# Large transfers moved to ACT's DMA queue, casting loads cut into pieces, in a transformer block on 8 cores

## The chip, the cores and the metric

One Trainium2 chip, 8 cores, the same program on each. Each core has its own 2 of the 16 sequences and its own copy of the weights; there is no exchange between cores. The metric is device microseconds of the slowest core. TensorE (PE), its weight load (PEld), VectorE (DVE), ScalarE (ACT), GpSimd (POOL) and SyncE (SP) each run their own instructions in order; SP only issues transfers. Sixteen DMA engines per core move the data.

## What is computed

One layer on x of [16, 2048, 1024] in float32:

```python
qkv = einsum('btc,fc->btf', x, w_qkv)                  # 16 heads of 64
p = softplus(einsum('bhqd,bhkd->bhqk', q, k) / 8)
p = p * p * causal
attn = p / (sum(p, -1) + 1e-9)
x = layernorm(x + einsum('btc,oc->bto', attn @ v, w_proj) + b_proj)
h = gelu(lora(x, quant(W_fc), b_fc, A_fc, B_fc))       # 1024 -> 4096
x = layernorm(x + lora(h, quant(W_proj), b_proj, A_proj, B_proj))
```

`quant` rounds a weight to 8 bits by its largest absolute value, and `lora` adds 2 * (x A^T) B^T. The kernel merges the LoRA product into the rounded weight.

## The kernel before

**Two halves.** The first half is attention for both sequences of a core, output projection and first layernorm (LN). The second is the FFN, matmul behind matmul on PE. In the first half the work goes by units: a unit is one block of keys against 512 queries for a pair of heads. Scores go to PSUM (L740), ACT applies softplus (L751), POOL masks the diagonal blocks (L758), DVE squares (L766), and the AV matmuls (L790) of unit u - 3 follow the scores of unit u. The sum over keys comes out of the same matmuls by a column of ones in V.

**The tick.** The order is written by hand. The main loop emits for each unit u: its scores and softplus, the square of unit u - 2, held evacuations, `run_due()` (one tick: what `after_ticks(n, fn)` has put off until now), then `pump`, which emits a share of the other PE work, and the AV of unit u - 3. A window is the 36 units of one pair of heads, `window(gp)`, gp 0 to 15 (14 and 15 are one). Its list of chains holds: Q and K of the next pair (ch_qk, L367, evacuated by ACT, L377), V (ch_v, L391), in windows 0 to 4 the absolute maxima of the weights (do_absmax, L467), in windows 5 to 13 the rounding and merging of the weights, which go back to HBM in bf16 (merge_half, L546 and L551), in window 8 the output projection of the first sequence, from window 14 on that of the second (ch_proj, L682). The end of window 4 holds do_scale and do_lora, a serial chain over the scales.

**Normalization** (emit_norm). When a group of 512 queries is done, ACT (L804) and DVE (L807) copy it from PSUM to `a_nd`. Then, at fixed ticks after that: SP fetches the sums to `g_den` (+2, L822), DVE takes the reciprocal (+5, L829 and L831), SP puts it to HBM (`recscr`, +6, L834), SP spreads it over the partitions (`a_bc`, +8, L841), and DVE scales into `a_QO` (+11, L849). All four transfers are small.

**ch_proj(n)** handles 128 rows: it adds PSUM to a tile of x in one of four slots of `g_x`. Its order is: `x_load(n + 1)`, 8 matmuls, add, `x_load(n + 2)`, `x_bias(n + 1)` on POOL (L616), 8 matmuls, add, `ln_finish(n - 1)`, `ln_stats(n)`. `ln_finish` scales on ACT (L649) and stores the tile twice: float32 to `x1scr` by SP (L658) and bf16 to `x1bscr` by POOL (L663, it casts). `x_load(n)` takes the slot of tile n - 4 and waits until both of its stores have landed.

**Queues.** Each engine's queue is in order, waits included. Before, SP issues every transfer that doesn't cast, POOL every one that does. Casting loads are wqk (one per window), wv (four), xT (four at the start, four in window 6) and wo (one, load_late, in window 1). Weight tiles (`w_load`, L444) go through six slots, later three; `w_take` has `w_fill` called four ticks later. `ffn_loads` in window 14 issues four `Wfc` loads, three `Wp` loads and the transposing loads of `x1bscr` (L952), one tick apart.

## Time and profile before

| what | us |
|---|---|
| three runs, slowest core | 2158.59, 2168.69, 2391.7 |
| median | 2168.69 |
| the profiled execution, its own time | 2155.1 |
| its span (core 1, the slowest) | 2153.4 |
| spans of the other cores | 2119.3 to 2139.2 |
| PE busy | 1920.0 (89%) |
| DVE, ACT, POOL busy | 991.1, 891.2, 453.6 |

The span is cut below into stages. The windows of the kernel begin where a 36th, 72nd, ... softplus (L751) starts, and the stages are cut there: 118.0 is the start of window 1, 194.5 of window 2, 314.3 of window 4, 384.3 of window 5, 441.1 of window 6, 614.6 of window 8, 811.7 of window 10, 1059.9 of window 14, 1143.5 of window 15. From 1290.4 on there is only the FFN. Busy times are sums over an engine's instructions; idle time in front of an instruction is put down to what released it last.

### The profile page before, as it was taken

How to read it: one execution, taken by the hardware profiler on the slowest of the kernel's cores; microseconds unless marked ns; L12 is line 12 of the kernel's file. 1: busy time of each engine (PE TensorE's matmuls, PEld its weight loads, DVE VectorE, ACT ScalarE, POOL GpSimd, SP SyncE). 2: the span in 40 equal slices, each digit the busy share in tenths (PEclk: the TensorE clock that was granted, in tenths of full speed). 3: DMA queues.
4: the chain of work that ended last, by engine and by line, in shares of the span. 5: the costliest groups of instructions: out<-in, count | busy, mean ns of one | idle time of the engine just before them, and what ended most of it. 6: DMA issues, size and time to landing. Idle time of an engine off the chain costs nothing.

```text
span 2153.4 us, 27198 instructions; the slowest of 8 cores (2119.3 to 2153.4 us)
## 1 busy us (share of the span) xinstructions
PE 1920.0 (89%) x8834; PEld 758.0 (35%) x8834; DVE 991.1 (46%) x1581; ACT 891.2 (41%) x1058; POOL 453.6 (21%) x549
## 2 busy tenths in 40 slices
PE   6897896877987888998968789999999999999998
PEld 2332332222322333332322234444444444444443
DVE  2675887765766688888747621111010102020202
ACT  2565675664434566667645431222212131313030
POOL 2121221221155512122227420101010101020201
PEclk9998999998999999999979899999999999999999
DMA  7657674557476544455276464020211111110101
GB/s 130 172 140 145 151 148 104 114 113 143 109 191 181 143 120 121 124 127 149 75 200 182 124 225 141 30 69 30 59 40 49 49 49 49 50 59 17 62 10 49
DMA packets 140842, 228.39 MB, mean 106 GB/s; under 512 B 77746, under 2 KB 78002, under 8 KB 138130
## 3 DMA queue, kind: packets, MB, share of 16 engines
q1 hardware_dynamic: 131570, 195.03, 32.4%
q0 software_dynamic: 9136, 31.63, 9.2%
q8 instruction: 75, 1.23, 0.3%
q14 instruction: 61, 0.50, 0.1%
HBM read 182.21 MB, written 58.98 MB: 112 GB/s over the span
## 4 chain that ended last, share of the span: by engine, by line
PE 61%; DMA 19%; DVE 7%; issue 5%; SPq 3%; POOL 2%; ACT 2%; DVEq 0%; POOLq 0%; ACTq 0%
PE ps_s L999 19%; PE ps_a L1051 10%; PE ps_f L1051 10%; DMA recscr<-g_rec 6%; PE ps_f L367 6%; PE ps_a L790 5%; DMA g_den<-a_nd 4%; PE ps_s L740 4%; PE ps_f L391 4%; DMA a_bc<-recscr 4%; DMA x1bscr<-g_x 2%; DVE a_ph L766 2%; PE ps_f L546 1%; PE ps_f L682 1%; ACT a_ph L751 1%
## 5 line engine op out<-in xcount | busy, mean ns | idle before, releaser
L751 ACT ACTIVATE a_ph<-ps_s 128x1024 bf16<-128x1024 f32 (+1 forms) x576 | 560.8, 977 | 446.3 <-PE ps_s L740 443.8
L1006 ACT ACTIVATE b_h<-ps_s,g_bfc,g_scl 128x512 bf16<-128x512 f32 x256 | 199.1, 779 | 631.0 <-PE ps_s L999 631.0
L999 PE MATMUL ps_s<-b_xT,b_Wfc 128*128 128x512 bf16 x2048 | 446.3, 380 | 6.2 <-ACT b_h L1006 6.2
L790 PE MATMUL ps_a<-a_ph,a_V 128*128 128x512 bf16 (+7 forms) x1280 | 350.9, 363 | 107.9 <-DVE a_ph L766 49.6
L766 DVE TENSOR_TENSOR a_ph<-a_ph 128x1024 bf16<-128x1024 bf16 (+1 forms) x576 | 402.7, 724 | 33.6 <-ACT a_ph L751 16.4
L367 PE MATMUL ps_f<-a_xT,a_wqk 128*128 128x512 bf16 x1024 | 300.3, 395 | 23.1 <-DMA a_xT<-xT 13.6
L758 POOL TENSOR_TENSOR a_ph<-a_ph,g_mask 128x256 bf16<-128x256 bf16 x256 | 198.7, 793 | 474.5 <-ACT a_ph L751 473.4
L1056 DVE SCALAR_TENSOR_TENSOR g_x<-ps_a,g_scl,g_x 128x512 f32<-128x512 f32 x32 | 24.0, 751 | 585.1 <-PE ps_a L1051 585.1
L999 PEld LDWEIGHTS ps_s<-b_xT,b_Wfc 128*128 128x128 bf16 x2048 | 200.9, 98 | 250.0 <-issue 10.2
L740 PE MATMUL ps_s<-a_QO,a_K 64*128 64x512 bf16 (+3 forms) x1280 | 225.4, 365 | 2.8 <-ACT a_QO L377 2.5
L1051 PE MATMUL ps_a<-b_Wp,b_h 128*128 128x512 bf16 x1024 | 224.4, 379 | 0.0
L1051 PE MATMUL ps_f<-b_Wp,b_h 128*128 128x512 bf16 x1024 | 223.6, 379 | 0.0
L790 PEld LDWEIGHTS ps_a<-a_ph,a_V 128*128 128x128 bf16 (+1 forms) x1280 | 131.0, 109 | 261.2 <-issue 162.8
L631 POOL TENSOR_SCALAR g_mv<-g_mv 128x1 f32<-128x1 f32 x64 | 15.5, 242 | 774.0 <-DVE g_mv L629 772.2
L391 PE MATMUL ps_f<-a_wv,a_xT 128*128 128x512 bf16 x512 | 145.2, 397 | 25.2 <-DVE a_V L400 14.2
L682 PE MATMUL ps_f<-a_wo,a_QO 128*128 128x512 bf16 x512 | 133.1, 401 | 38.1 <-DVE g_x L688 23.9
L616 POOL TENSOR_TENSOR g_x<-g_x,g_bias 128x1024 f32<-128x1024 f32 x64 | 151.2, 2363 | 42.3 <-DMA g_x<-x 30.9
L1051 PEld LDWEIGHTS ps_a<-b_Wp,b_h 128*128 128x128 bf16 x1024 | 99.7, 98 | 122.1 <-issue 3.3
L1051 PEld LDWEIGHTS ps_f<-b_Wp,b_h 128*128 128x128 bf16 x1024 | 100.1, 98 | 120.9
L740 PEld LDWEIGHTS ps_s<-a_QO,a_K 64*128 64x128 bf16 x1280 | 57.0, 93 | 226.8 <-issue 226.8
L849 DVE TENSOR_TENSOR a_QO<-a_nd,a_bc 64x512 bf16<-64x512 f32 x128 | 93.3, 729 | 92.7 <-DMA a_bc<-recscr 82.9
L367 PEld LDWEIGHTS ps_f<-a_xT,a_wqk 128*128 128x128 bf16 x1024 | 76.3, 99 | 153.7 <-issue 113.5
(52 smaller groups left out, 926.0 us busy)
## 6 DMA issues: line engine op xcount, KB each, us to landing
a_w<-wfc SPq DMA_DIRECT2D x49, 512.0 KB, 6.1
a_w<-wpF SPq DMA_DIRECT2D x48, 512.0 KB, 5.4
a_bc<-recscr SPq DMA_DIRECT2D x128, 128.0 KB, 4.5
g_x<-x SPq DMA_DIRECT2D x32, 512.0 KB, 4.8
x1scr<-g_x SPq DMA_DIRECT2D x32, 512.0 KB, 5.3
g_x<-x1scr SPq DMA_DIRECT2D x32, 512.0 KB, 3.3
out<-g_x SPq DMA_DIRECT2D x32, 512.0 KB, 2.6
g_x<-wpF SPq DMA_DIRECT2D x16, 512.0 KB, 6.4
```

What stands on the lines that cost most here:

```text
L367: tok = P.op("tensor", lambda E, cc=cc: E.matmul(ps, a_wqk[:, (gp % 2) * 2048 + which * 1024 + cc * 128: (gp % 2) * 2048 + which * 1024 + ...
L391: tok = P.op("tensor", lambda E, cc=cc: E.matmul(ps, a_xT[:, tg * 4096 + cc * 512 + (tt % 4) * 128: tg * 4096 + cc * 512 + (tt % 4 + 1) * ...
L616: x_tok[n] = P.op("gpsimd", lambda E: E.tensor_tensor(g_x[:, sl * 1024:(sl + 1) * 1024], g_x[:, sl * 1024:(sl + 1) * 1024], g_bias[:, :], ...
L682: tok = P.op("tensor", lambda E, cc=cc, q0=q0, ps=ps, oh=oh: E.matmul(ps, a_QO[:, q0:q0 + 128], a_wo[:, cc * 1024 + oh * 512: cc * 1024 + ...
L740: tok = P.op("tensor", lambda E, kc=kc, c0=c0, n=n, hd=hd, b0=b0: E.matmul(ps_s[:, b0:b0 + n], a_K[hd * 64:hd * 64 + 64, (gp % 2) * 2048 + ...
L751: s_read[sl] = P.op("scalar", lambda E: E.activation(dst, src, AF.Softplus, scale=HS ** -0.5), waits=[tok, ph_av[q]])
L758: sp_tok[u] = P.op("gpsimd", lambda E, off=off: E.tensor_tensor(ph[:, :, off:off + 128], ph[:, :, off:off + 128], mk, ALU.mult), waits=[s_ ...
L766: sq_tok[u] = P.op("vector", lambda E: E.tensor_tensor(ph[:, :, 0:n], ph[:, :, 0:n], ph[:, :, 0:n], ALU.mult), waits=[sp_tok[u]])
L790: tok = P.op("tensor", lambda E, c0=c0, n=n, off=off, lhs=lhs, rows=rows, hd=hd, fin=fin: E.matmul(ps_a[0:rows, hd * 512 + c0: hd * 512 + ...
L999: tok = P.op("tensor", lambda E, cc=cc, c0=c0: E.matmul(ps, b_Wfc[:, c0:c0 + 128], b_xT[:, (g % 2) * 4096 + cc * 512:(g % 2) * 4096 + (cc ...
L1006: h_tok[(g, f)] = P.op("scalar", lambda E: E.activation(b_h[:, f * 512:(f + 1) * 512], ps, AF.Gelu, bias=g_bfc[:, f:f + 1], scale=g_scl[:, ...
L1051: tok = P.op("tensor", lambda E, k=k, f=f, ps=ps, tc=tc, oh=oh: E.matmul(ps, b_h[:, f * 512 + tc * 128: f * 512 + (tc + 1) * 128], b_Wp[:, ...
```

## The change

Three things. Transfers of the weights' float32 tiles (from the seventh on), the stores of the merged weights, the loads of x and the stores of `x1scr`, the loads of `Wfc`, three of the `Wp` loads and the bias are issued by ACT in place of SP. The casting loads are issued in 4, 8 or 16 pieces, most of them some ticks apart. The stores of a finished tile are put off by one tick, or until `x_load` needs their slot, and `w_fill` comes after five ticks in place of four. SP keeps the small transfers of the normalization, the transposing loads, the rest of `Wp`, and the loads and stores of the second half.

```diff
         k_wv = {}
         k_xT = {}
 
-        def load_wqk(gp, after=()):
+        def in_parts(sem, dst, src, n, step, after):
+
+            c = dst.shape[1] // n
+            end = sem.n + 16 * n
+
+            def part(i):
+                P.dma("gpsimd", sem, lambda E: E.dma_start(
+                    out=dst[:, i * c:(i + 1) * c], in_=src[:, i * c:(i + 1) * c]),
+                    waits=after if i == 0 else ())
+
+            part(0)
+            for i in range(1, n):
+                if step:
+                    after_ticks(i * step, lambda i=i: part(i))
+                else:
+                    part(i)
+            return (sem, end)
+
+        def load_wqk(gp, after=(), n=1, step=0):
             pr, sl = gp % NP, gp % 2
-            k_wqk[(gp, 0)] = k_wqk[(gp, 1)] = P.dma("gpsimd", msem(f"wqk{sl}"), lambda E: E.dma_start(
-                out=a_wqk[:, sl * 2048:(sl + 1) * 2048], in_=d_wqk[pr, :, :]), waits=after)
+            k_wqk[(gp, 0)] = k_wqk[(gp, 1)] = in_parts(
+                msem(f"wqk{sl}"), a_wqk[:, sl * 2048:(sl + 1) * 2048], d_wqk[pr, :, :], n, step, after)
         def load_first():
 
...
             rows(1)
             part(1)
 
-        def load_wv(s, hf, after=()):
-            k_wv[(s, hf)] = P.dma("gpsimd", msem("wv"), lambda E: E.dma_start(
-                out=a_wv[:, :], in_=d_wv[hf, :, :]), waits=after)
-
-        def load_xT(s, tg, after=()):
-            k_xT[(s, tg, 0)] = k_xT[(s, tg, 1)] = P.dma("gpsimd", msem(f"xT{tg}"), lambda E: E.dma_start(
-                out=a_xT[:, tg * 4096:(tg + 1) * 4096], in_=d_xT[s, tg, :, :]), waits=after)
+        def load_wv(s, hf, after=(), n=1, step=0):
+            k_wv[(s, hf)] = in_parts(msem("wv"), a_wv[:, :], d_wv[hf, :, :], n, step, after)
+
+        def load_xT(s, tg, after=(), n=1, step=0):
+            k_xT[(s, tg, 0)] = k_xT[(s, tg, 1)] = in_parts(
+                msem(f"xT{tg}"), a_xT[:, tg * 4096:(tg + 1) * 4096], d_xT[s, tg, :, :], n, step, after)
         load_first()
         load_wv(0, 0)
...
                 out=a_lo1[0:16, :], in_=d_afc)))
             k_lo.append(P.dma("gpsimd", msem("apj"), lambda E: E.dma_start(
                 out=a_lo2[32:48, :], in_=d_apj)))
-            k_wo.append(P.dma("gpsimd", msem("wo"), lambda E: E.dma_start(out=a_wo[:, :], in_=d_wo)))
-            k_bias.append(P.dma("sync", msem("bias"), lambda E: E.dma_start(
+            k_wo.append(in_parts(msem("wo"), a_wo[:, :], d_wo, 16, 4, ()))
+            k_bias.append(P.dma("scalar", msem("bias"), lambda E: E.dma_start(
                 out=g_bias[:, :], in_=d_bo.broadcast_to([128, C]))))
 
...
             src, p0, pn = w_src[k]
             sl = w_slot(k)
             w_busy[sl] = True
-            w_tok[k] = P.dma("sync", msem(f"w{sl}"), lambda E: E.dma_start(
+            w_tok[k] = P.dma("sync" if k < 6 else "scalar", msem(f"w{sl}"), lambda E: E.dma_start(
                 out=w_tile(k)[p0:p0 + pn, :], in_=src), waits=[w_free[sl], k_xT[(0, 3, 0)]])
         def w_take(k):
             w_fill(k)
-            after_ticks(4, w_fill)
+            after_ticks(5, w_fill)
             return w_tile(k)
         def w_fill(upto=None):
...
                 def store():
                     if stores.pop(i, None) is None:
                         return
-                    wb_st[sl] = P.dma("sync", msem(f"wb{sl}"), lambda E: E.dma_start(
+                    wb_st[sl] = P.dma("scalar", msem(f"wb{sl}"), lambda E: E.dma_start(
                         out=dst, in_=a_wb[:, sl * 1024:(sl + 1) * 1024]), waits=[tb])
                     wq_st[i] = wb_st[sl]
 
...
         xb_st = {}
         ln_wait = {}
         slot_out = [[], [], [], []]
+        stored = set()
+        to_store = {}
         def x_load(n):
 
...
             sl = n % 4
             t = n % NT
             src = d_x if n < NT else d_x1
+            if n >= 4:
+                to_store[n - 4]()
             w = list(slot_out[sl])
             if n >= NT:
                 w.append(x_st[t])
             if n < 4:
                 w.append(scl_tok[0])
-            x_dma[n] = P.dma("sync", msem(f"x{sl}"), lambda E: E.dma_start(
+            x_dma[n] = P.dma("scalar" if n < NT else "sync", msem(f"x{sl}"), lambda E: E.dma_start(
                 out=g_x[:, sl * 1024:(sl + 1) * 1024], in_=src[t * 128:(t + 1) * 128, :]), waits=w)
         def x_bias(n):
...
                     ALU.subtract, ALU.mult), waits=[ln_wait.pop(n)])
             st_free[q] = ta
             dst = d_x1 if n < NT else d_out
-            st = P.dma("sync", msem(f"st{sl}"), lambda E: E.dma_start(
-                out=dst[t * 128:(t + 1) * 128, :], in_=x), waits=[ta])
-            slot_out[sl] = [st]
-            x_st[t if n < NT else n] = st
-            if n < NT:
-                xb_st[n] = P.dma("gpsimd", msem(f"xb{sl}"), lambda E: E.dma_start(
-                    out=d_x1b[t * 128:(t + 1) * 128, :], in_=x), waits=[ta])
-                slot_out[sl].append(xb_st[n])
+
+            def store():
+                if n in stored:
+                    return
+                st = P.dma("scalar" if n < NT else "sync", msem(f"st{sl}"), lambda E: E.dma_start(
+                    out=dst[t * 128:(t + 1) * 128, :], in_=x), waits=[ta])
+                slot_out[sl] = [st]
+                x_st[t if n < NT else n] = st
+                if n < NT:
+                    xb_st[n] = P.dma("gpsimd", msem(f"xb{sl}"), lambda E: E.dma_start(
+                        out=d_x1b[t * 128:(t + 1) * 128, :], in_=x), waits=[ta])
+                    slot_out[sl].append(xb_st[n])
+                stored.add(n)
+
+            to_store[n] = store
+            if n < NT - 1:
+                after_ticks(1, store)
+            else:
+                store()
         def ch_proj(n):
 
...
                     main += [ch_qk(0, 0, tg, 0), ch_qk(0, 0, tg, 1)]
                     main += [ch_v(0, 0, tg * 4 + i) for i in range(4)]
                 main.append(ch_do(("ld", 0), lambda: (
-                    load_wqk(2, after=[qk_pe[0]]), load_wv(0, 1, after=[v_pe[(0, 0)]]))))
+                    load_wv(0, 1, after=[v_pe[(0, 0)]], n=4, step=1), load_wqk(2, after=[qk_pe[0]], n=4, step=4))))
             if s == 1 and pr == 0:
                 main += [ch_proj(n) for n in range(16)]
             if gp == 14:
...
                         main += [ch_qk(s, pr + 1, tg, 0), ch_qk(s, pr + 1, tg, 1)]
                         if gp == 6:
                             main.append(ch_do(("ldx", tg), lambda tg=tg: load_xT(
-                                1, tg, after=[xT_pe[(0, tg)]])))
+                                1, tg, after=[xT_pe[(0, tg)]], n=4, step=2)))
             if pr in (1, 2, 3):
                 lo, hi = {1: (0, 5), 2: (5, 10), 3: (10, 16)}[pr]
                 extra += [ch_v(s, 1, tt) for tt in range(lo, hi)]
...
         def first_loads(gp):
             if gp >= 1 and gp + 2 < SEQ * NP:
-                load_wqk(gp + 2, after=[qk_pe[gp]])
+                load_wqk(gp + 2, after=[qk_pe[gp]], n=4, step=5)
             if gp == 4:
-                load_wv(1, 0, after=[v_pe[(0, 1)]])
+                load_wv(1, 0, after=[v_pe[(0, 1)]], n=8, step=4)
             if gp == 8:
-                load_wv(1, 1, after=[v_pe[(1, 0)]])
+                load_wv(1, 1, after=[v_pe[(1, 0)]], n=8, step=4)
         def ffn_loads():
             for fb in range(4):
...
         x1T_tok = {}
         def load_wfc(fb, after):
-            wfc_tok[fb] = P.dma("sync", msem(f"wfc{fb}"), lambda E: E.dma_start(
+            wfc_tok[fb] = P.dma("scalar", msem(f"wfc{fb}"), lambda E: E.dma_start(
                 out=b_Wfc[:, fb * 4096:(fb + 1) * 4096], in_=d_wfcb[fb, :, :]),
                 waits=list(after) + [wq_st[fb * 4 + i] for i in range(4)])
         def load_wp(f0, f1, after):
-            t = P.dma("sync", msem(f"wp{f0}"), lambda E: E.dma_start(
+            t = P.dma("scalar" if f0 in (26, 30, 14) else "sync", msem(f"wp{f0}"), lambda E: E.dma_start(
                 out=b_Wp[:, f0 * 1024:f1 * 1024].rearrange("p (f d) -> p f d", d=1024),
                 in_=d_wpb[f0:f1, :, :].rearrange("f p d -> p f d")),
                 waits=list(after) + [wq_st[32 + f] for f in range(f0, f1)])
```

## Rows read from the trace of the kernel before

**Rows 1.** The page: busy time by engine, and the chain by engine.

```profile
PE 1920.0 (89%) x8834; PEld 758.0 (35%) x8834; DVE 991.1 (46%) x1581; ACT 891.2 (41%) x1058; POOL 453.6 (21%) x549
...
PE 61%; DMA 19%; DVE 7%; issue 5%; SPq 3%; POOL 2%; ACT 2%; DVEq 0%; POOLq 0%; ACTq 0%
```

**Rows 2.** Stages: us, busy us (x instructions) of PE, PEld, DVE, ACT, POOL; PEclk; DMA.

```profile
118.00:194.50 76.50, 56.88 (x265) 19.13 (x266) 50.85 (x77) 40.88 (x48) 13.73 (x21) 0.89 0.68 154
194.50:256.00 61.50, 55.06 (x265) 18.71 (x264) 48.25 (x73) 40.89 (x49) 12.22 (x18) 0.97 0.56 131
...
314.30:384.30 70.00, 49.89 (x228) 15.23 (x227) 52.48 (x83) 40.36 (x49) 13.45 (x19) 0.90 0.52 117
384.30:441.10 56.80, 49.66 (x237) 16.36 (x236) 43.51 (x75) 40.25 (x50) 12.63 (x18) 0.97 0.51 108
441.10:517.70 76.60, 54.50 (x237) 16.79 (x236) 42.66 (x74) 40.36 (x50) 15.00 (x21) 0.84 0.67 124
...
614.60:747.20 132.60, 107.87 (x481) 40.82 (x480) 87.65 (x138) 59.22 (x63) 80.89 (x97) 0.94 0.64 166
...
811.70:878.60 66.90, 59.78 (x281) 20.73 (x280) 52.40 (x86) 40.89 (x49) 13.29 (x18) 0.97 0.49 119
...
1059.90:1143.50 83.60, 61.25 (x290) 21.86 (x289) 44.65 (x75) 43.95 (x54) 30.78 (x36) 0.84 0.62 158
1143.50:1226.40 82.90, 65.80 (x285) 22.42 (x283) 61.39 (x95) 46.25 (x47) 50.74 (x57) 0.90 0.58 156
...
1290.40:2153.40 863.00, 853.75 (x3944) 385.73 (x3944) 119.09 (x192) 186.67 (x240) 97.38 (x96) 0.99 0.16 51
```

**Rows 3.** Waits: us in total, times, longest.

```profile
DVE a_QO L849 <- DMA a_bc<-recscr: 82.9, 36, 10.1
...
DVE g_den L829 <- DMA g_den<-a_nd: 54.1, 14, 12.4
PE ps_a L790 <- DVE a_ph L766: 49.6, 29, 7.7
...
PE ps_s L740 <- ACT a_ph L751: 0.2, 1, 0.2
```

**Rows 4.** Timelines of SP, POOL and DVE around 455 us: start us, us.

```profile
443.72 0.42 SPq L444 DMA_DIRECT2D a_w<-wfc  x1
...
456.95 1.12 SPq L841 DMA_DIRECT2D a_bc<-recscr  x2
...
454.07 0.58 POOL L257 DMA_DIRECT2D a_xT<-xT  x1 [4.04 <-PE ps_a L790]
...
466.46 0.68 DVE L849 TENSOR_TENSOR a_QO<-a_nd,a_bc 64x512 bf16<-64x512 f32 x1 [7.85 <-DMA a_bc<-recscr]
```

**Rows 5.** DVE's timeline at 181 us, and the issues of a_wo.

```profile
181.58 0.17 DVE L829 TENSOR_SCALAR g_den<-g_den 128x8 f32<-128x8 f32 x1 [12.37 <-DMA g_den<-a_nd]
...
a_wo<-wo POOLq DMA_DIRECT2D x1, 2048.0 KB, 19.9
```

**Rows 6.** SP's timeline in window 14 and at the end.

```profile
1101.55 10.44 SPq L952 DMA_TRANSPOSE b_xT<-x1bscr  x1
...
1277.90 15.34 SPq L944 DMA_DIRECT2D b_Wp<-wpb  x4
```

**Rows 7.** SP's own waits: us in total, times, longest.

```profile
SPq L86 <- DMA x1scr<-g_x: 110.1, 26, 6.7
```

**Rows 8.** x1scr stores in windows 8 and 14 to 15; x1bscr landings, 640:732 and 1195:1199.

```profile
L658 SPq DMA_DIRECT2D x1scr<-g_x x15: 327/383/985, 627.2 to 732.4; - x15
...
L658 SPq DMA_DIRECT2D x1scr<-g_x x12: 319/329/1629, 1127.1 to 1216.6; - x12
...
DMA to landing us min/median/max: 3.3/6.3/8.0
...
DMA to landing us min/median/max: 3.7/3.7/3.7
```

## The prediction, made before the change was run

> **What bounds the kernel now.** I read four views in this order. The page says that PE is busy for 1920.0 us of 2153.4 and that 19% of the chain that ended last is DMA [rows 1]. So PE is the bound, except where something stalls it, and the stalls are transfers. The table by stage says where [rows 2]. From 1290.4 us on, the second half gives PE 853.75 busy us of 863.0; nothing of the change reaches it. All that can be won lies before. There stages that hold the same PE work take different times: the stage from 384.3 (window 5) and the one from 441.1 (window 6) both have 237 matmuls, but take 56.8 and 76.6 us. Windows 1 and 2 both have 265, and take 76.5 and 61.5.
>
> The waits say how a transfer reaches PE [rows 3]: DVE stands 82.9 us before L849 for `a_bc` and 54.1 us before L829 for `g_den`, and PE stands 49.6 us for a square (`a_ph` L766) that is queued on DVE behind these. The small transfers of the normalization have fixed due ticks (fetch +2, recip +5, put +6, spread_out +8, scale +11); a tick is 1.6 to 2.3 us (a stage over its 36 units), so three ticks give a transfer some 5 to 7 us.
>
> Last, two places show why they come late. In window 6 a casting load of `xT` starts at 454.07, `a_bc` is issued at 456.95, 13 us after SP's last weight load, and DVE waits 7.85 us for it until 466.46 [rows 4]. In window 1 the 2 MB cast of `wo` holds DVE for 12.37 us until 181.58 [rows 5].
>
> **The change, part by part.** The sum is against the profiled execution, 2155.1 us (span 2153.4).
>
> Casting loads in pieces: the same bytes in 86 more issues. The `wo` load: window 1 costs 76.5 - 61.5 = 15.0 us over window 2 [rows 2]. The one load takes 19.9 us to land [rows 5]; a sixteenth of it is 1.2 us, and with a fixed part as large as the shortest landing of a store (3.7 [rows 8]) a piece is through in 5 us, inside the three ticks. I take 12 of the 15.0, since other waits of window 1 stay. The four `xT` loads: window 6 over window 5, 76.6 - 56.8 = 19.8 us. A piece of 256 KB every 2 ticks leaves small transfers to pass, but the same bytes must still go through; I take 14 (bounds 0 and 19.8). `wv(1,0)` in window 4: 70.0 - 56.8 = 13.2 us, but that stage holds the serial chain of do_scale and do_lora too, which stays; I take 4 (0 to 8). The 86 issues cost POOL 0.58 us each [rows 4], 50 us in all on an engine busy 453.6 us [rows 1]; a mask can come 0.6 us later. Two units stand between a softplus and its square, which hide it; without that cover it would be 50 us, and I take nothing.
>
> The large hardware transfers leave SP's queue: 127 weight loads, 64 stores of cast weights, 32 loads and 32 stores of `g_x`, 8 of `Wfc`, 3 of `Wp` and the bias, 267 in all. SP's fetches no longer stand behind them or behind their waits. In window 14 (`Wfc`, `Wp` and the first transposes) 290 matmuls take 83.6 us, where window 10 takes 66.9 for 281 [rows 2], 16 us of excess. There SP stands 10.44 us in the first DMA_TRANSPOSE [rows 6], behind `Wfc` and `Wp`. The bytes keep their size and place, so I take 6 (0 to 15). For the rest (windows 0, 7, 9 to 13, where the small transfers share a queue with weight loads) I take 12, bounded by 0 and 20. That is well under the 137.0 us that DVE waits, of which PE sees a part only, since window 10 (66.9 us, 281 matmuls) takes no more for a matmul than window 5. Gain: 12 + 14 + 4 + 6 + 12 = 48 us.
>
> For what a second queue does there is no row, since before only SP and POOL issue. The nearest is [rows 4], where a transfer of another queue (POOL's) delays SP's fully. The Trainium skill ("DMA: Bandwidth & Descriptors", "Issuing engines are not separate DMA queues") says so too: issuing from several engines only saves the issue time. Its section "Queues, rings and completion order" has each DMA engine take packets from the rows of the grid in turn, which would let a 2 KB fetch overtake. By the first rule the last two terms, 18 us, go; by the second they stay. No row tells these apart.
>
> What ACT takes on. An issue occupied SP 0.33 to 0.38 us in the median [rows 8]: 267 x 0.4 = 107 us of ACT's queue, beside 891.2 - 186.67 = 704.5 busy us in 1290 [rows 1, 2]. That is still under two thirds, and PE runs up to three units ahead of the softplus it needs: nothing, at most 20. Behind each such issue on ACT stand the next softplus, the evacuations at L377 and L804 and the LN scaling at L649. The weight loads wait for `w_free`, a DVE operation some two ticks old when they are issued; PE's own AV matmul of that tick already waits for squares as young. So I cost that wait at 0 to 5, and take 0.
>
> **The wait that is moved.** `x_load(n + 2)` in the middle of ch_proj must wait until the stores of tile n - 2 have landed. SP does that today, 110.1 us in 26 waits for `x1scr` [rows 7]. Now ACT does. And the store is put off by a tick, so that it comes directly ahead of that load, with no ACT work between: ACT stands for the whole landing. POOL's half of the store also moves behind the g_mv operations of the next tile. How long is the landing? 6.3 us in the median where the next load runs beside it, 3.7 where nothing large does [rows 8]. Since the load can no longer start before the store has landed, the two don't overlap, and 3.7 is the nearer row; with 0.5 us for POOL's turn I take B = 4.2. In window 8 a tile takes (732.4 - 627.2) / 14 = 7.5 us [rows 8], and ACT is busy 59.22/132.6 of that, 3.35 us. New: 3.35 + 0.8 for issues + 4.2 = 8.35 us, so ACT sets the pace: + 0.85 x 14 = 12 us. In windows 14 and 15 a tile takes (1216.6 - 1127.1) / 11 = 8.1 us and ACT is busy 46.25/82.9 of it, 4.5 us; 4.5 + 0.8 + 4.2 = 9.5, + 1.4 x 11 = 15, of which I take 10, because these tiles also stand before gates (`after` on o_tok) in which ACT catches up. The last four tiles, with gelus behind them: + 3. A loss of 25 us, with bounds 0 (B of 3.3 or less) and 65 (B of 6.3: 0.85 + 2.1 more on 14 tiles, 3.5 on 11, less some gate time).
>
> Net: 48 - 25 = 23 us, so 2132 for an execution like the profiled one. Of the three runs the lower two are 2158.6 and 2168.7, their middle is 2163; the forecast for a median is **2163 - 23 = 2140 us**.
>
> **Rivals.**
> (a) Forecast, both effects as sized: 2110 to 2165. Chance 0.42.
> (b) The small transfers come on time and the block on ACT is hidden by the three units that PE may run ahead (11 us at the 132.6/36 = 3.7 us of a tick in window 8): 15.0 + 19.8 + 8 + 15 + 20 = 78 us gained, nothing lost: 2085. For it speaks that the excess of window 6 over window 5 is so clean; against it, that ACT's work for a tile plus the landing is more than a tile's time now, which no run-ahead can hide. Chance 0.28.
> (c) A second queue buys nothing, since it is the 16 DMA engines that are shared, as [rows 4] has it; only the pieces help: 12 + 14 + 4 - 25 = 5 us, 2158. This is what the skill's rule named above would give. Against it: [rows 6], where SP itself was held. Chance 0.18.
> (d) Slower: ACT blocks longer than one landing, in ch_proj. The place is x_load behind to_store, the price 25 tiles x (B - 3.3). The gain is gone at B = 5.2, and 2% slower (43 us) needs 25 x (B - 3.3) = 48 + 43, B = 6.9. The landings under load reach 8.0 us [rows 8], so it is possible; at B = 8.0 it is 118 - 48 = 70 us, 2233. Ring backlog adds to it: four issues of `Wp` in a row occupied SP for 15.34 us [rows 6], and on ACT it would hold softplus. Chance 0.12.
>
> **How the numbers follow.** Likeliest is (a), 2140. About 2% is what a measurement of this kernel tells from no change: 2125 and 2212. Faster by more: (b), and the lower part of (a), 0.10: 0.38. Slower: (d), 0.12. Within: 0.50. The range goes from (b) at 2085 to 2190, between (c) with all of ACT's small costs (20 + 5) and (d); it leaves out a fifth.
>
> **What would show it.** Window 6 should come to some 60 us against 56.8 of window 5, and window 1 near window 2; the long waits for `g_den` and `a_bc` should be gone before 600 us, and DVE's waits on them halved in sum. The first transpose should be issued in 5 us. In windows 8, 14 and 15 ACT should show a wait of about 4 us behind each store of `x1scr`, with PE waiting for ACT at L740, where today that is 0.2 us in all [rows 3], and a tile of 8.3 us. The second half should not move. Wrong would be: waits of DVE for `a_bc` unchanged (then (c)), tiles over 10 us (then (d)), or tiles at 7.5 or under (then (b)).

## The result, and the profile after

The changed kernel takes 2271.47 us in the median (2249.59 to 2293.32) against 2163.64 before: slower, by a ratio of 1.0476 with a 95% interval of 1.0359 to 1.0592. The forecast was 2140 us, and the range 2085 to 2190. In the profiled executions of the changed kernel and of weights_only below, the cores of one die were slowed down, so of these two I compare only the four cores of the other die; of the changed kernel I read core 6, whose span is 2228.8 us.

The page of the changed kernel (its slowest core): busy time, queues, chain.

```profile
PE 1951.3 (85%) x8660; PEld 765.9 (33%) x8834; DVE 1005.5 (44%) x1581; ACT 887.0 (39%) x1058; POOL 502.4 (22%) x635
...
q10 hardware_dynamic: 38528, 125.65, 19.4%
q1 hardware_dynamic: 93042, 69.38, 11.7%
q0 software_dynamic: 21520, 31.63, 10.3%
...
PE 58%; DMA 22%; DVE 7%; issue 5%; POOL 3%; ACT 3%; SPq 1%; ACTq 0%; DVEq 0%; POOLq 0%
```
PE's share of the chain is 58% where it was 61% [rows 1], DMA's 22% for 19%. A new queue q10 carries ACT's 125.65 MB, and POOL's q0 has 21520 packets for the same 31.63 MB.

The table by stage of core 6, cut at the same softplus as before: windows 1, 2, 4 to 8, 10, 14, 15 and the FFN.

```profile
132.40:203.40 71.00, 58.75 (x265) 19.55 (x266) 48.42 (x73) 41.00 (x48) 15.47 (x25) 0.88 0.58 132
203.40:264.00 60.60, 54.61 (x265) 18.81 (x264) 50.30 (x75) 41.06 (x49) 18.49 (x30) 0.97 0.71 159
...
330.30:399.30 69.00, 48.71 (x228) 15.05 (x227) 51.78 (x82) 40.15 (x48) 18.04 (x29) 0.95 0.54 120
399.30:456.10 56.80, 49.85 (x237) 16.50 (x236) 43.80 (x74) 40.23 (x50) 14.14 (x21) 0.97 0.48 103
456.10:525.00 68.90, 56.01 (x237) 16.59 (x236) 44.00 (x74) 40.43 (x49) 22.05 (x33) 0.85 0.66 133
525.00:637.90 112.90, 88.74 (x377) 29.93 (x376) 66.04 (x109) 41.49 (x49) 16.75 (x26) 0.89 0.44 108
637.90:799.40 161.50, 117.50 (x481) 43.04 (x480) 90.83 (x138) 57.04 (x63) 86.40 (x108) 0.86 0.60 152
...
864.20:928.80 64.60, 58.05 (x281) 20.34 (x280) 52.62 (x86) 40.93 (x49) 14.93 (x21) 1.00 0.48 123
...
1119.60:1209.50 89.90, 64.72 (x302) 23.27 (x301) 49.75 (x80) 43.94 (x54) 34.14 (x40) 0.85 0.57 156
1209.50:1301.10 91.60, 69.66 (x273) 22.30 (x271) 64.99 (x94) 45.43 (x47) 47.42 (x53) 0.83 0.51 139
...
1386.60:2228.80 842.20, 829.74 (x3841) 375.10 (x3839) 119.04 (x192) 174.90 (x225) 94.67 (x94) 0.99 0.15 47
```
Against [rows 2]: window 6 takes 68.9 us for 76.6, but window 7 takes 112.9 us, window 8 161.5 for 132.6, windows 14 and 15 89.9 and 91.6 for 83.6 and 82.9. PE's clock in window 8 falls from 0.94 to 0.86.

One core's windows vary by some 10 us, so from here on I compare medians over the eight cores of a profile (four for "changed" and weights_only), in us; the runs with ratios follow below. "14-15" ends with the last softplus, and the tail lies between that and the first matmul of the FFN's second product.

| kernel | 0 | 1-3 | 4-6 | 7 | 8 | 9-13 | 14-15 | tail | FFN |
|---|---|---|---|---|---|---|---|---|---|
| before | 115 | 188 | 195 | 95 | 131 | 315 | 166 | 89 | 839 |
| changed | 126 | 192 | 195 | 119 | 160 | 321 | 183 | 85 | 842 |
| x_only | 115 | 191 | 196 | 94 | 163 | 324 | 187 | 90 | 839 |
| x_nodelay | 113 | 187 | 193 | 94 | 152 | 314 | 173 | 87 | 839 |
| pieces_only | 113 | 211 | 197 | 100 | 142 | 332 | 173 | 90 | 842 |
| pieces_at_once | 112 | 190 | 196 | 94 | 133 | 318 | 167 | 90 | 843 |
| weights_only | 123 | 197 | 197 | 120 | 133 | 330 | 174 | 90 | 839 |
| wload_act | 119 | 194 | 201 | 99 | 130 | 328 | 169 | 89 | 839 |
| wload_pool | 120 | 188 | 197 | 100 | 135 | 335 | 168 | 91 | 843 |
| wstore_act | 115 | 188 | 190 | 132 | 130 | 322 | 170 | 89 | 839 |
| nonorm_before | 112 | 163 | 166 | 92 | 126 | 311 | 143 | 81 | 839 |
| nonorm_weights | 112 | 163 | 170 | 110 | 126 | 312 | 145 | 81 | 839 |
| late_not7 | 112 | 178 | 190 | 95 | 131 | 309 | 168 | 89 | 839 |

The changed kernel's loss sits in window 8 (+29), window 7 (+25), windows 14 and 15 (+17), window 0 (+12) and windows 9 to 13 (+6).

Waits of core 6 in the changed kernel: us in total, times, longest.

```profile
ACT a_ph L783 <- DMA x1bscr<-g_x: 90.1, 15, 9.1
...
DVE a_QO L881 <- DMA a_bc<-recscr: 66.5, 32, 12.7
...
DVE g_den L861 <- DMA g_den<-a_nd: 43.9, 14, 11.9
...
PE ps_s L772 <- ACT a_ph L783: 34.0, 18, 5.1
...
PE ps_a L822 <- ACT a_nd L836: 22.2, 7, 7.0
...
DVE a_wb L568 <- DMA wfcb<-a_wb: 15.1, 6, 4.0
```
PE's 0.2 us for ACT [rows 3] has become 34.0, and its waits for the copy `a_nd` on ACT are 22.2 us. On core 6 before, that wait was:

```profile
PE ps_a L790 <- ACT a_nd L804: 7.5, 2, 5.6
```
A stretch of window 8 shows how (timeline of core 6 of the changed kernel: start, us; the idle time before and what ended it in brackets).

```profile
711.69 0.33 ACTq L683 DMA_DIRECT2D x1scr<-g_x  x1
...
715.42 0.54 POOL L688 DMA_DIRECT2D x1bscr<-g_x  x1
...
719.53 0.33 ACTq L627 DMA_DIRECT2D g_x<-x  x1
719.96 0.60 ACT L783 ACTIVATE a_ph<-ps_s 128x512 bf16<-128x512 f32 x1 [7.44 <-DMA x1bscr<-g_x]
...
721.59 0.58 ACT L836 ACTIVATE a_nd<-ps_a 65x512 f32<-65x512 f32 x1
...
722.31 1.03 PE L822 MATMUL ps_a<-a_ph,a_V 128*65 128x512 bf16 x2 [6.99 <-ACT a_nd L836]
```
ACT issues the store of `x1scr` at 711.69 and can issue the load into that slot only at 719.53, when both halves of the store have landed. Here POOL issues its half only at 715.42, behind pieces of `wqk` and `wv` and its own operations, so that about half of ACT's stand is POOL's turn. The next softplus had to wait 7.44 us, the copy of `ps_a` behind it is done at 722.2, and PE, which has run its units ahead by then, stands 6.99 us.

### The profile page after: what moved, and what is told of

The parts are those of the page before. It is cut to its first block, busy times and chain, and to the rows that moved or that the text cites. A ratio compares the mean times of both kernels' runs of the same rounds, so it can differ in the third digit from the quotient of the medians.

```text
span 2291.7 us, 27111 instructions; the slowest of 8 cores (2213.5 to 2291.7 us)
## 1 busy us (share of the span) xinstructions
PE 1951.3 (85%) x8660; PEld 765.9 (33%) x8834; DVE 1005.5 (44%) x1581; ACT 887.0 (39%) x1058; POOL 502.4 (22%) x635
## 3 DMA queue, kind: packets, MB, share of 16 engines
q10 hardware_dynamic: 38528, 125.65, 19.4%
q1 hardware_dynamic: 93042, 69.38, 11.7%
q0 software_dynamic: 21520, 31.63, 10.3%
## 4 chain that ended last, share of the span: by engine, by line
PE 58%; DMA 22%; DVE 7%; issue 5%; POOL 3%; ACT 3%; SPq 1%; ACTq 0%; DVEq 0%; POOLq 0%
PE ps_s L1031 18%; PE ps_a L1083 10%; PE ps_f L1083 10%; DMA recscr<-g_rec 7%; PE ps_a L822 5%; PE ps_f L384 5%; DMA a_bc<-recscr 5%; PE ps_f L408 4%; PE ps_s L772 4%; DMA x1bscr<-g_x 4%; DMA g_den<-a_nd 3%; DVE a_ph L798 2%; ACT a_ph L783 2%; PE ps_f L714 1%; DMA wfcb<-a_wb 1%
## 5 line engine op out<-in xcount | busy, mean ns | idle before, releaser
L822 PE MATMUL ps_a<-a_ph,a_V 128*128 128x512 bf16 (+7 forms) x1260 | 358.6, 373 | 135.4 <-DVE a_ph L798 57.8
L798 DVE TENSOR_TENSOR a_ph<-a_ph 128x1024 bf16<-128x1024 bf16 (+1 forms) x576 | 413.9, 743 | 70.1 <-ACT a_ph L783 41.4
L772 PE MATMUL ps_s<-a_QO,a_K 64*128 64x512 bf16 (+3 forms) x1280 | 231.2, 374 | 41.9 <-ACT a_ph L783 35.4
L714 PE MATMUL ps_f<-a_wo,a_QO 128*128 128x512 bf16 x499 | 142.2, 430 | 27.5 <-DVE a_QO L881 13.3
```

The source lines that it names most:

```text
L714: tok = P.op("tensor", lambda E, cc=cc, q0=q0, ps=ps, oh=oh: E.matmul(ps, a_QO[:, q0:q0 + 128], a_wo[:, cc * 1024 + oh * 512: cc * 1024 + ...
L772: tok = P.op("tensor", lambda E, kc=kc, c0=c0, n=n, hd=hd, b0=b0: E.matmul(ps_s[:, b0:b0 + n], a_K[hd * 64:hd * 64 + 64, (gp % 2) * 2048 + ...
L798: sq_tok[u] = P.op("vector", lambda E: E.tensor_tensor(ph[:, :, 0:n], ph[:, :, 0:n], ph[:, :, 0:n], ALU.mult), waits=[sp_tok[u]])
L822: tok = P.op("tensor", lambda E, c0=c0, n=n, off=off, lhs=lhs, rows=rows, hd=hd, fin=fin: E.matmul(ps_a[0:rows, hd * 512 + c0: hd * 512 + ...
```

## The experiments

Theory W said that this wait costs; the rival, Q, was that ACT's queue is burdened by the issues, or the DMA engines by the pieces. The first four runs each undo or do one part.

**x_only** (1.0159, 1.0095 to 1.0223) and **all_but_x** (1.0322, 1.0258 to 1.0386).

```diff
 # x_only: before.py with
-x_dma[n] = P.dma("sync", ...)         # and the store of x1scr
+x_dma[n] = P.dma("scalar" if n < NT else "sync", ...)
+if n < NT - 1: after_ticks(1, store)
 # all_but_x: after.py with both on "sync", store() at once
```

> The kernel before, with the loads of x and the stores of x1scr on ACT's queue and the stores put off by a tick; weights and casting loads as before. Theory W (the wait for the stores' landing, moved to ACT, is what costs): windows 8, 14 and 15 take on what the changed kernel shows there over the kernel before, 30.6, 10.6 and 8.2 us (medians of the cores), all other stages stay, so 45 to 55 us slower, a ratio of 1.021 to 1.026, with ACT waiting 60 us or more for x1bscr in window 8. Rival Q (ACT's queue is burdened by issues of weights and stores, or the DMA engines by the pieces): under 15 us slower, a ratio under 1.007.

> The changed kernel, with the loads of x and the stores of x1scr back on SP's queue and not put off; all else as changed. Theory W: windows 8, 14 and 15 return to 131, 82 and 83 us; what is left is window 7 (+24 us), window 0 (+10) and windows 3 and 5 (+9), so 35 to 50 us slower than before, 1.016 to 1.023. Rival Q: 80 us or more slower, a ratio of 1.037 or more. My forecast before the result, had it been right but for x: 48 us faster, 0.978.

x_only has all of the changed kernel's loss in windows 8, 14 and 15 (163 and 187 us for 131 and 166), and 9 us in windows 9 to 13, which W had at nothing. It loses 35 us by the ratio, under the 45 to 55 of theory W, but mostly where W said. all_but_x has window 8 at 141 and windows 14 and 15 at 170, but is slower than W allowed, 1.032 for at most 1.023, and faster than the 1.037 of Q. So the x part is one cause of several.

**pieces_only** (1.0182, 1.0113 to 1.0252) and **weights_only** (1.0256, 1.0195 to 1.0317).

```diff
 # pieces_only: before.py with in_parts(...) in load_wqk, load_wv, load_xT and for wo
 # weights_only: before.py with
-w_load, store of a_wb, load_wfc, three load_wp, bias: P.dma("sync", ...)
+P.dma("scalar", ...)
-after_ticks(4, w_fill)
+after_ticks(5, w_fill)
```

> The kernel before with the casting loads in pieces, all else as before. Theory S (pieces spare the small transfers): windows 1, 2 and 6 take 25 us less in sum, nothing is lost, ratio 0.985 to 0.99. Theory C (the same bytes delay the small transfers as much, for longer, as window 6 of the changed kernel says, 69.9 against 70.9 us): windows 1, 2 and 6 gain under 6 us, ratio 0.995 to 1.005. A loss in window 7 of over 10 us would put its 24 us down to the pieces of xT and wv that run into it.

> The kernel before with the weights' tiles, their merged stores, Wfc, three Wp loads and the bias on ACT's queue and the refill a tick later; x and casting loads as before. Theory A (ACT's queue makes stores and refills late where merges are dense): window 7 takes 15 to 24 us more, window 0 up to 10 more, ratio 1.01 to 1.018, with DVE waiting for wfcb in window 7 for 12 us instead of 6.6. Rival (issues on ACT are free, as I took them, and SP's freed queue helps): window 7 stays, windows 9 to 14 gain 10 to 18 us, ratio 0.99 to 0.995.

Neither theory on the pieces held: they are slower by themselves, in windows 1 to 3 (+23), 8 (+10) and 9 to 13 (+17). The weights' queue loses 26 us in window 7 and 9 in window 0, about as theory A had it, but also 15 in windows 9 to 13 and 9 each in windows 1 to 3 and 14 and 15, so that the ratio is over the 1.018 of theory A. The three parts don't add up: 1.6, 1.8 and 2.6% are 6.0%, and the whole loses 4.8%. Pieces and weights together (all_but_x) lose 3.2% where they would sum to 4.4%; which wait they share wasn't looked into.

**Delay, spreading, ticks, loads and stores apart.** **x_nodelay** (1.0112, 1.0058 to 1.0165) is x_only with `store()` at once. **pieces_at_once** (1.0122, 1.0063 to 1.018) is pieces_only with all pieces of a load issued together. **wload_act** (1.0166, 1.0098 to 1.0234) has only w_load on "scalar", **wstore_act** (1.0153, 1.008 to 1.0225) only the stores of `a_wb`. **weights_tick4** (1.0301, 1.0224 to 1.0379) is weights_only with `after_ticks(4, w_fill)`.

```diff
 # x_nodelay: x_only with
-after_ticks(1, store)
+store()
 # pieces_at_once: pieces_only with
-if step:
+if False:
 # wload_act: before.py with
-w_tok[k] = P.dma("sync", ...)
+w_tok[k] = P.dma("sync" if k < 6 else "scalar", ...)
 # wstore_act: before.py with
-wb_st[sl] = P.dma("sync", ...)
+wb_st[sl] = P.dma("scalar", ...)
 # weights_tick4: weights_only with
-after_ticks(5, w_fill)
+after_ticks(4, w_fill)
```

> x_only (1.016) without the delay of the stores by a tick: the store of a tile is issued at once after its scaling, on ACT, its load still waits there. Theory D (the delay puts the whole landing on ACT): the softplus that now lies between store and load, and the 8 matmuls, cover about half of the landing, so window 8 falls from 163 us to about 145 and the ratio to 1.005 to 1.01. Rival (ACT waits for the landing either way, as SP did): window 8 stays at 155 us or more, ratio 1.013 or more.

> pieces_only (1.018) with the same pieces issued one right behind the other, so the smaller rows and the extra issues stay and the spreading over ticks goes. Theory P (spreading keeps some cast in flight beside nearly every small transfer; recscr has 2.45 large ones beside it in place of 1.73): DVE's waits for a_bc fall from 106 us toward 71, ratio 1.0 to 1.006. Rival R (smaller rows cost the DMA engines more, q0 has 21520 packets for 9136): it stays slow, ratio 1.012 or more. Either way the 3 us at the end stay, where POOL's last drain takes 9.2 us for 6.0.

> The weights on ACT's queue as in weights_only (1.026), but the refill of weight slots after four ticks again, not five. Theory K (the later refill makes the loads late in window 7): window 7 falls from 123 to about 105 us, ratio 1.015 to 1.02. Theory A (it is ACT's queue that issues stores and loads late, behind softplus): window 7 stays at 118 to 125 us, ratio 1.022 to 1.03.

> The kernel before with only the loads of weight tiles (from the seventh) on ACT's queue, refill after four ticks, stores of the merged weights on SP. Theory A1 (the refill is late, since ACT comes to it only behind the softplus of its tick): window 7 takes most of the 28 us that weights_only shows there, ratio 1.012 to 1.02. Theory A2 (the late stores are it; DVE waited 19.5 us for wfcb and 12.7 for a_w): window 7 under 105 us, ratio under 1.008.

> The kernel before with only the 64 stores of the merged weights on ACT's queue. wload_act left window 7 at 99 us on the median core where weights_only has 123, so theory A2 puts the rest on the stores: ACT issues one only behind the softplus of its tick, and DVE waits for its slot two tiles later. Then window 7 takes 112 us or more and all else stays, ratio 1.008 to 1.014. If window 7 stays under 102, it takes both together.

x_nodelay: the delay is worth 11 us in window 8 and 14 in windows 14 and 15; the wait without it still costs 21 us in window 8. Both expectations missed (152 us, between 145 and 155, and a ratio between 1.01 and 1.013). Waits in x_only, and in x_nodelay below it:

```profile
ACT a_ph L783 <- DMA x1bscr<-g_x: 82.9, 14, 8.6
...
PE ps_s L772 <- ACT a_ph L783: 36.1, 15, 7.8
```
```profile
ACT a_ph L780 <- DMA x1bscr<-g_x: 48.8, 11, 5.8
...
PE ps_s L769 <- ACT a_ph L780: 26.0, 14, 5.0
```
pieces_at_once: the stages return to within 5 us of before, so it is the spreading that costs there, with DVE's waits for `a_bc` at 85.5 us on the average core (106.3 in pieces_only, 71.3 before). The ratio stayed at 1.012 all the same. The mean span of the eight cores in its one profile (2151.2 us for 2134.6) is 0.8% over before, which is inside the interval of the ratio; some 4 us of it are at the end of the second half. So the spreading is shown for windows 1 to 3 and 8 to 13, and what the pieces cost even at once is less sure.

weights_tick4: window 7 stays at 120 us, so the later refill was not the cause. wload_act leaves window 7 at 99 on the median core, wstore_act takes it to 132: **it is the stores**, in window 7. (The stores alone cost more there than stores and loads together, 132 for 120; why stays open.) Core 0 of wstore_act in window 7, timeline:

```profile
562.09 0.33 ACTq L582 DMA_DIRECT2D wfcb<-a_wb  x1
...
566.38 0.69 DVE L568 SCALAR_TENSOR_TENSOR a_wb<-a_w,ps_f 128x512 bf16<-128x512 f32 x1 [4.35 <-DMA wfcb<-a_wb]
...
567.22 1.87 PE L408 MATMUL ps_f<-a_wv,a_xT 128*128 128x512 bf16 x4 [4.45 <-DVE g_den L858]
...
570.58 1.02 ACT L780 ACTIVATE a_ph<-ps_s 128x1024 bf16<-128x1024 f32 x1 [7.05 <-PE ps_s L769]
...
574.34 0.33 ACTq L582 DMA_DIRECT2D wfcb<-a_wb  x1
```
The same in the kernel before (core 7): the merge's last operation, then the store.

```profile
531.20 0.69 DVE L551 SCALAR_TENSOR_TENSOR a_wb<-a_w,ps_f 128x512 bf16<-128x512 f32 x1 [0.29 <-PE ps_f L546]
...
531.96 0.33 SPq L565 DMA_DIRECT2D wfcb<-a_wb  x1
...
540.34 0.69 DVE L551 SCALAR_TENSOR_TENSOR a_wb<-a_w,ps_f 128x512 bf16<-128x512 f32 x1 [0.44 <-PE ps_f L546]
...
541.92 0.46 SPq L565 DMA_DIRECT2D wfcb<-a_wb  x1
```
Before, SP issues the store 0.1 to 0.9 us after DVE's addition has ended, here. ACT comes to it only behind the softplus of its tick, DVE waits 4.35 us for the slot, PE 4.45 for DVE, ACT stands 7.05 us before its next softplus, and with it the next store is late. Over all tiles whose merge ends in window 7, on all cores, the time from the end of a merge to the issue of its store has a median of 2.8 us before, 7.9 in wstore_act and 8.1 in weights_only; its least is 0.1 us before and 5.5 in both others. The code says why: the store is put off by `after_ticks(4, store)`, before and after, or until the merge two tiles later needs its slot. SP, which follows no softplus, can stand at that place when the data come; ACT reaches it after the softplus of these ticks. That fewer ticks would cure it on ACT is not shown, since no run changes them.

**What the small transfers are worth, and what disturbs them.** **nonorm_before** (0.9424, 0.9346 to 0.9502) and **nonorm_weights** leave out the four small transfers of the normalization.

```diff
-st[hd] = P.dma("sync", ...)    # fetch, put and spread_out alike
+st[hd] = k_one2                # token of a memset to 1.0
```

> The kernel before without the four small transfers of the normalization: their tiles are set to 1 once, so the output isn't normalized, and DVE does all its operations still. It gives the ceiling of what any freeing of these transfers can win. My sum took 48 us for it and put the bound at 78; DVE waits 117 us for them on the average core. Theory L (much of it reaches PE): 50 to 80 us faster, 0.965 to 0.977. Rival (PE's idle time was due to DVE's load and only fell to these waits): under 25 us faster, 0.989 or more.

> weights_only without the same four small transfers (output not normalized). If weights_only loses its 2.6% through the small transfers, which now run beside large ones that SP's queue used to hold back (recscr lands in 4.5 us instead of 3.3, DVE waits 168 us for a_bc and g_den instead of 117), it is as fast as nonorm_before, within 10 us. If it loses through late stores and loads of the merges, it stays 25 to 40 us slower than nonorm_before, all of it in windows 0 and 7.

The ceiling is 5.8%, 125 us, half again over what theory L allowed. I had summed PE's idle time, but the clock comes on top. Up to the FFN's second product PE is idle for 206 us before and 130 without the small transfers (medians of the cores), and busy for 1089 us before and 1060 without them, with the same number of matmuls. So some 75 us are idle time, and some 29 lie in the matmuls, which ran at a higher clock: the mean granted clock of the slowest core is 0.979, and before it is 0.961. nonorm_weights took 2067.4 and 2073.6 us where nonorm_before took 2037.2 to 2039.6, 33 us more by the medians, with 18 us of it in window 7 and 3 in windows 4 to 6. So, by subtraction, of the 56 us of weights_only some 33 go through the merges and some 23 through the small transfers.

Why do the small transfers suffer, when large ones leave their queue? **wload_pool** (1.0111, 1.0018 to 1.0204) puts the weight loads on "gpsimd" with semaphores of their own. **hold** (1.0213, 1.0145 to 1.0281) adds the token of the last small transfer to the waits of w_load and of the stores, on SP. **hold_late** (1.0184, 1.0114 to 1.0255) does that with later ticks.

```diff
 # wload_pool: before.py with
-w_tok[k] = P.dma("sync", msem(f"w{sl}"), ...)
+w_tok[k] = P.dma("sync" if k < 6 else "gpsimd", ...)  # own semaphores
 # hold: before.py with small[:] = the last small transfers' tokens
-waits=[w_free[sl], k_xT[(0, 3, 0)]])           # w_load
+waits=[w_free[sl], k_xT[(0, 3, 0)]] + small)
-waits=[tb])                                    # store of a_wb
+waits=[tb] + small)
 # hold_late: hold with after_ticks of 6, 7, 9 and 13 for 5, 6, 8 and 11
```

> The kernel before with the loads of weight tiles (from the seventh) on POOL's queue, where little else stands; ACT issues nothing. Theory T (the small transfers lose because large ones now come from another queue than theirs, whichever: they start while the small ones are in flight and share with them): DVE's waits for a_bc rise from 71 us to over 90, as with ACT (96), ratio 1.01 or more. Theory A (it is ACT's in-order queue and what it delays): a_bc waits stay under 80 us and the ratio within 0.995 to 1.005.

> The kernel before, where each load of a weight tile and each store of a merged one on SP also waits until the small transfer issued last has landed. Theory T turned round: SP's queue protects the small transfers because it stands in their waits and keeps large ones back, and more of it helps: DVE's waits for a_bc and g_den fall from 117 us to under 95, 5 to 25 us faster, 0.988 to 0.998. Rival: large transfers ahead of the small ones matter, not those behind: waits unchanged, and refills come later, 1.0 to 1.01.

> hold together with the later ticks of before_late2 (recip +6, put +7, spread_out +9, scale +13). If both mechanisms are right they add: a_bc waits under 45 us, windows 1, 2 and 6 at 60, 56 and 62 us, 20 to 35 us faster than before, 0.984 to 0.991. If window 7 pays with late refills (it took 101.5 us in before_late2 and 94.5 before), the gain is under 10 us.

The landing of `recscr` on core 6, before, in weights_only and in wload_pool:

```profile
DMA to landing us min/median/max: 1.6/3.6/15.2
```
```profile
DMA to landing us min/median/max: 1.6/4.5/16.7
```
```profile
DMA to landing us min/median/max: 1.5/4.2/11.8
```
Over all cores these medians are 3.3 us before, 4.5 in weights_only, 3.9 in wload_pool and 4.0 in wload_act. wload_pool behaves like wload_act (`a_bc` waits of 86.7 and 96.3 us on the average core): ACT's queue isn't needed for this loss. That SP protects the small ones by holding large ones back was not borne out: hold did hold them back (0.20 large transfers issued during a flight of `recscr`, 0.87 before), yet `recscr` landed in 3.5 us, no sooner than before, and the waits for `a_bc` rose to 101.5 us, those for `g_den` from 45.5 to 59.5. hold is no clean test, though: SP stands in the added waits itself, and small transfers behind them come later. hold_late was to add up two gains and came out 1.8% slower, with windows 1 to 3 at 199 us and window 7 at 120.

What is left is a count over all cores, by how many large transfers were in flight when `recscr` was issued. Its median time to landing:

| large ones in flight | before | wload_act | wload_pool |
|---|---|---|---|
| none | 2.7 us (220) | 2.6 (184) | 2.7 (155) |
| one | 3.5 (174) | 3.9 (149) | 4.0 (198) |
| two | 5.5 (60) | 5.6 (120) | 5.3 (97) |
| three or more | 7.0 (58) | 7.8 (59) | 7.1 (62) |

What changes most is how often two or more are in flight: 118 times of 512 before, 179 in wload_act, 159 in wload_pool (and 186 in pieces_only, 126 in pieces_at_once). Whose queue they come from matters less. With exactly one ahead and none issued behind, one of SP's own cost 3.4 us (69 times, before), one of ACT's 3.1 (38, wload_act), one of POOL's 4.1 (46, wload_pool). So with the loads on another queue more large transfers overlapped. It is a count, not a controlled run: the transfers' sizes and their places in the program differ between the groups, and the cause of this part of the loss stays argued.

**ffn_only** (1.0, 0.9954 to 1.0047) has only `Wfc`, three `Wp` and the bias on ACT.

```diff
-load_wfc, three load_wp, bias: P.dma("sync", ...)
+P.dma("scalar", ...)
```

> The kernel before with only the eight loads of Wfc, three of Wp and the bias on ACT's queue. I had given it 6 us of gain in window 14, since SP no longer stands 10.44 us in its first transpose. Theory T (a large load ahead in another queue delays a small one more than one ahead in its own): window 14 takes 84 to 90 us instead of 82.4, ratio 1.0 to 1.005. If SP's stand was the cost: window 14 at 74 to 78 us, ratio 0.996 to 0.998.

Window 14 took 83.7 us (82.4 before): no gain, no loss. SP's stand in the first transpose did get shorter, 8.5 us for 11.7 on the median core, and nothing came of it.

**Beyond the kernel before.** **before_late** (0.9993, 0.9945 to 1.0041) moves recip, put and scale to +6, +7, +13; **before_late2** also spread_out to +9; **late_not7** (0.9913, 0.9878 to 0.9947) leaves windows 7, 14 and 15 out of it.

```diff
 # before_late: before.py with 6, 7, 8, 13; before_late2: with 6, 7, 9, 13
 # late_not7:
+k = int(gp not in (7, 14, 15))
-after_ticks(5, recip)  # 6 put, 8 spread_out, 11 scale
+after_ticks(5 + k, recip)  # 6 + k, 8 + k, 11 + 2 * k
```

> The kernel before with more ticks for the small transfers: recip at +6 in place of +5, put at +7 in place of +6, scale at +13 in place of +11, nothing moved between queues. Theory L: it gives each wait of DVE 2 to 4 us more and takes most of them away, 20 to 45 us faster, 0.98 to 0.99. Rival: the two buffers are held longer and the end of attention comes later, no gain, 0.995 to 1.005.

> before_late (0.999) with spread_out at +9 in place of +8. There windows 1 to 6 gained 17 us and window 7 lost 18, which I read so: put at +7 and spread_out at +8 left SP waiting for recscr with the merges' loads and stores behind it. If so, window 7 returns to 95 to 100 us and windows 1 to 6 keep their gain: 15 to 25 us faster, 0.988 to 0.993. If window 7 stays at 110 us or more, the later ticks themselves disturb it, ratio 0.997 to 1.003.

> The kernel before with the later ticks of before_late2 in all windows but 7, 14 and 15. There windows 1, 2 and 3 took 181 us for 191 before and window 7 took 101.5 for 94.5; with window 7 spared it should be 5 to 12 us faster than before, 0.994 to 0.998. If DVE's waits are not what PE loses there, it is 1.0 within 0.003.

before_late gained 15 us in windows 1 to 6 and gave 18 back in window 7; before_late2 (2135.6 and 2160.1 us, before 2154.6 to 2169.8) still gave 7 back and stays inconclusive. late_not7 spares windows 7, 14 and 15 and is **faster than both kernels**, by 0.9% against before, where 0.2 to 0.6% was expected. The gain is in windows 0 to 6 (17 us) and 9 to 13 (6). Its waits on its slowest core, where [rows 3] had 82.9 and 54.1:

```profile
DVE a_QO L849 <- DMA a_bc<-recscr: 58.3, 21, 6.8
...
DVE g_den L829 <- DMA g_den<-a_nd: 40.8, 13, 13.2
```
On the average core only the waits for `a_bc` fell, from 71 to 47 us; those for `g_den` stayed at 45.

## Why the prediction was wrong

The forecast had a gain of 48 us and a loss of 25. Of the gain nothing came, and the loss was larger and had a second source that the sum put at nothing.

**The wait that is moved** was the right mechanism with a size too small. It is the first half of my rival (d), which had 0.12. From the issue of a store to that of the load of its slot it takes 6.0 us in the median of the eight cores (5.8 on cores 4 to 7), where I took B = 4.2. Before, on SP, it was 6.3. The 3.7 us in B rested on the landing of a single store of `x1bscr`, and it was not the shortest either: [rows 8] has 3.3. In the changed kernel POOL's half is issued 1.4 us behind ACT's, where I took 0.5, and then takes 4.1 to land, with casts and small transfers beside it. The loss in windows 8 and 14 and 15 was 31 and 21 us in x_only, and 29 and 17 in the changed kernel, not 12 and 10. That a tile takes 8.7 us in window 8 (forecast 8.35) and 9.7 in window 14 on (forecast 9.5) is partly luck: my formula, ACT's work plus issues plus B, gives 3.35 + 0.8 + 5.8 = 9.95 for window 8, so it overstates the tile where B understates the wait. Of the 29 us of window 8, by the times of the adds to `g_x`, 17 are the tiles. The first add comes 5 us later after the window's start, and 7 are what follows the last add, the Q and K chains behind the projection. I had priced the tiles alone. And (d) doesn't explain the result either: by its own price, 25 x (5.8 - 3.3) = 63 us less the gain of 48, the kernel would be 15 us slower, and it is some 100.

**"So I cost that wait at 0 to 5, and take 0"** is the step that failed outright. It asked how long ACT waits for its semaphores, and that was small (1 to 6 us for `a_wb` on a core of the changed kernel). It did not ask how late a transfer is issued when its queue moves in step with the softplus, where SP ran ahead and issued a store soon after its data were there. The stores alone cost 38 us in window 7 (wstore_act). No rival had this.

**The second queue's 18 us** (6 and 12 for windows 14 and the rest) have the wrong sign: windows 9 to 13 lose 13 to 20 us with the weights' loads on either other queue, ffn_only gains nothing. [rows 4] had shown a transfer of another queue delaying SP's, and I gave rival (c) 0.18. Of the two statements of the Trainium skill ("DMA: Bandwidth & Descriptors") that the prediction names, "Issuing engines are not separate DMA queues" fits this case better, since no gain came; that moving them would lose, neither says. The turn-taking that the Trainium skill has in the same page under "Queues, rings and completion order" let no 2 KB fetch overtake in a way that the medians show (3.3 us before, 3.2 in weights_only).

**The pieces' 30 us** did not come either. Windows 1 and 2 took 132 us in the changed kernel for 134 before and window 6 68 for 71. Spreading means that a cast is nearly always in flight: 2.45 large transfers lay beside a flight of `recscr` in pieces_only, 1.73 before. That the small transfers make the excess was right: without them window 6 takes 54.3 us for the 55.7 of window 5, and windows 1 and 2 take 53.6 each. That pieces cure it was wrong. And [rows 2] is core 1, which had the dearest window 6 of the eight; the median core had 15 us of excess there, not 19.8. The 15.0 us of window 1 over window 2 stood on three cores only: on the other five window 1 was the shorter one, by 6 to 11 us.

**The second half**, which I said would not move, lost 3 us (839 to 842), in POOL's last instruction (below).

**Right** were ACT's waits behind each store, PE's wait at L740, and that ACT's queue had room for the issues themselves (0.33 us each).

## What to carry to other kernels

Before you move a transfer to a compute engine's queue, ask where that queue stands when the data are ready, not how long the issue takes: here SP issued a store 2.8 us after its data, ACT, in step with its own work, 7.9 us after, and a wait for a landing stops all of ACT's work. A stall's price includes the clock that it loses PE (here some 29 us beside 75 of idle time), so a run without the suspect (here 5.8%) sizes it better than the sum of idle times. Read an excess on all cores before you price it; I had read two on core 1 alone. To cut waits for small transfers, more ticks between issue and use gained 0.9%, where every move of the weights or of x to another queue, but for ffn_only's, lost 1 to 3%.

## What the runs showed of the hardware

The last DRAIN of POOL, at the end of the execution, was longer where POOL had issued more transfers. Core 6 before (65 issues) and in pieces_only (151):

```profile
L102 POOLq DRAIN  x1: 5982/5982/5982, 2131.7 to 2131.7; - x1
```
```profile
L102 POOLq DRAIN  x1: 9167/9167/9167, 2158.1 to 2158.1; - x1
```
That is 3.2 us for 86 more issues, the 3 us of the second half. It isn't the bytes, which are 31.63 MB in both; packets (9136 and 21520) and issues grow together. The count of issues alone doesn't set it: with the same 151 issued at once it is 9.8 us, and in wload_pool, with 192, 10.1.
